# First stage of a fused block: expansion split around the next tile's transposes, ScalarE's and VectorE's order changed

## The reference

```
x = x + tanh(g_xattn[0]) * xattn0(layernorm(x), ctx)     # per tile: scores = k^T q / 16, softmax, times v^T
h = layernorm(x)
z = h @ ternary(W_syn).T + b_syn                          # 128 x 1024 per tile
thresh = 102nd largest z of each row
hidden = where(z >= thresh, relu(z), 0)
x = x + tanh(g_ffn[0]) * (layernorm(h + hidden @ ternary(W_out).T + b_out) * gamma + beta)
x = x + tanh(g_xattn[1]) * xattn1(...)                    # convolution by Toeplitz matrices
x = x + tanh(g_ffn[1]) * mixture_of_experts(...)          # 64 experts, 6 per row
```

## Time and profile before

| what | us |
|---|---|
| median of three runs | 753.64 |
| the profiled execution, device time | 755.16 |
| its span (first to last instruction) | 753.0 |
| first expansion starts | 32.90 |
| second expansion starts | 41.84 |
| twelfth expansion starts | 104.82 |
| last expansion ends | 130.65 |
| threshold search on VectorE starts from the counts | 138.7 |

### The profile page before, as it was taken

One profiled execution on the slowest core, in us unless ns is written; L12 is line 12 of the kernel. 1 busy time (PEld: TensorE's weight loads), 2 busy tenths in 40 slices (PEclk: granted clock), 3 DMA queues, 4 the chain that ended last, 5 costly groups with the idle time before them and its releaser, 6 DMA issues.

```text
span 753.0 us, 12159 instructions
## 1 busy us (share of the span) xinstructions
PE 620.4 (82%) x3072; PEld 475.3 (63%) x3072; DVE 478.6 (64%) x1604; ACT 284.2 (38%) x641; POOL 433.4 (58%) x482
## 2 busy tenths in 40 slices
PE   3698997475699867799999658999999999999930
PEld 2354553243687755677777546788888888888720
DVE  4887777899587777778888352444444535354425
ACT  2135667785134341344555402223332323232200
POOL 2477888321044441377777660667777777777660
PEclk9599999788799997899999978999999999999975
DMA  6347553586568946466764368999999999998858
GB/s 227 109 161 235 190 195 138 194 301 249 200 248 317 328 168 222 159 211 226 247 235 144 125 219 275 288 249 243 245 250 252 245 253 259 260 256 171 228 85 308
DMA packets 89035, 167.84 MB, mean 223 GB/s; under 512 B 11280, under 2 KB 53712, under 8 KB 88976
## 3 DMA queue, kind: packets, MB, share of 16 engines
q1 hardware_dynamic: 67504, 138.44, 55.2%
q0 software_dynamic: 20608, 27.82, 18.8%
q10 hardware_dynamic: 864, 0.93, 0.3%
HBM read 93.33 MB, written 73.81 MB: 222 GB/s over the span
## 4 chain that ended last, share of the span: by engine, by line
PE 63%; DVE 13%; issue 8%; DMA 7%; POOL 3%; ACT 3%; SPq 1%; DVEq 1%; POOLq 0%; ACTq 0%
PE psum L1100 10%; PE psum L863 8%; PE psum L1018 6%; PE psum L1113 6%; PE psum L939 5%; PE psum L1104 5%; PE psum L1084 3%; PE psum L1118 3%; DMA acc<-hh,toki 3%; PE psum L1029 3%; DVE hh L1650 3%; PE psum L975 2%; POOL acc L806 2%; PE psum L835 2%; PE psum L930 2%
## 5 line engine op out<-in xcount | busy, mean ns | idle before, releaser
L806 POOL DMA_INDIRECT acc<-hh,toki x128 | 187.9, 1468 | 83.3 <-DVE hh L1965 47.8
L1965 DVE TENSOR_SCALAR hh<-psum,wtok 96x256 f32<-96x256 f32 (+3 forms) x128 | 55.9, 478 | 133.4 <-issue 113.2
L766 POOL DMA_INDIRECT xs_rows<-Z,slot x96 | 96.3, 1003 | 41.9 <-issue 26.0
L1100 PE MATMUL psum<-qT,Z 128*128 128x192 f32 (+3 forms) x480 | 99.3, 350 | 0.0
L1100 PEld LDWEIGHTS psum<-qT,Z 128*128 128x128 f32 x480 | 81.8, 192 | 3.0 <-issue 0.2
L684 POOL TENSOR_TENSOR rstd<-mv,neghalf 128x1 f32<-128x1 f32 (+1 forms) x48 | 36.8, 767 | 77.5 <-DVE mv L1438 77.5
L1375 ACT ACTIVATE qT<-psum 128x384 f32<-128x384 f32 (+3 forms) x64 | 33.5, 524 | 97.0 <-PE psum L1084 96.2
L863 PE MATMUL psum<-wt,hTs 128*128 128x512 f32 x128 | 62.0, 629 | 8.2 <-ACT hTs L1198 8.2
L939 PE MATMUL psum<-wt,hh 128*128 128x256 f32 x256 | 58.4, 382 | 0.0
L1113 PE MATMUL psum<-Z,hh 128*96 128x256 f32 (+3 forms) x240 | 56.7, 379 | 0.0
L1104 PE MATMUL psum<-qT,Z 128*112 128x192 f32 (+3 forms) x240 | 53.5, 345 | 0.0
(11 more groups left out here) (347 smaller groups left out, 1254.0 us busy)
## 6 DMA issues: line engine op xcount, KB each, us to landing
Z<-in_wexp SPq DMA_DIRECT2D x62, 496.0 KB, 4.3
xs_rows<-fill SPq DMA_DIRECT2D x64, 272.0 KB, 3.2
kv_rows<-Z SPq DMA_DIRECT2D x12, 688.0 KB, 3.8
kvb<-kv_rows SPq DMA_DIRECT2D x8, 688.0 KB, 5.6
Z<-co_rows SPq DMA_DIRECT2D x8, 688.0 KB
Z<-kv_rows SPq DMA_DIRECT2D x8, 688.0 KB, 6.4
Z<-xs_rows SPq DMA_DIRECT2D x24, 204.0 KB, 4.2
Z<-xs_rows SPq DMA_DIRECT2D x16, 272.0 KB, 3.7
```

What stands on the lines that cost most here:

```text
L766: pool.indirect_dma_start(out=xs_rows[:, :], out_offset=bass.IndirectOffsetOnAxis(ap=slot[:, t, k:k + 1], axis=0), in_=H[:, t, :], in_offs ...
L806: pool.indirect_dma_start(out=acc[a][:, :], out_offset=bass.IndirectOffsetOnAxis(ap=toki[0:p, g, j:j + 1], axis=0), in_=y_sb[0:p, s, j, :] ...
L1100: m = pe.matmul(pA[par][:, g * CAP:g * CAP + 2 * p], w[:, s, k, g * P:(g + 1) * P], xT[:, par, k, 0:2 * p], start=(k == 0), stop=(k == 1))
L1965: m = dve.tensor_scalar(y_sb[0:p, s, j, :], pY[par][0:p, j * D:(j + 1) * D], wtok[0:p, g, j:j + 1], None, ALU.mult)
```

## The change

TensorE's expansion of a tile becomes two calls: its first half (columns 0 to 511) stays at the head of the block, its second half goes behind the transposes of the next tile. ScalarE runs X, then C, then EH, with the counts for one tile later than before, and the counts left over follow the loop. On VectorE the instructions stay the same; `link` is taken apart, so that the wait for a result can stand later than the instruction that makes it (`mark` returns the number to wait for), and the block's order is new.

```diff
-            def expand(b, par):
-                pe.wait_ge(hT_ready, b + 1)
-                if later(b):
-                    pe.wait_ge(z_ready, b - 1)
-                for c in range(2):
-                    for k in range(2):
...
+            def expand(b, par, c):
+                if c == 0:
+                    pe.wait_ge(hT_ready, b + 1)
+                    if later(b):
+                        pe.wait_ge(z_ready, b - 1)
+                for k in range(2):
...
+                if c == 1:
+                    m.then_inc(z_done, 1)
...
                 if there(b - 3):
-                    expand(b - 3, 1 - par)
+                    expand(b - 3, 1 - par, 0)
...
                     turn(b - 2, par)
+                if there(b - 3):
+                    expand(b - 3, 1 - par, 1)
...
+            def counts(t):
...
+                first_count(t)
+                if t:
+                    second_count(t - 1)
+
+            for b in range(NT + 2):
+                if b < NT:
+                    soft(b, b % 2)
...
                 if b >= 5:
-                    second_count(b - 5)
...
+                    counts(b - 5)
+                if b >= 2:
+                    evac_h(b - 2, b % 2)
+            for t in range(NT - 3, NT):
+                counts(t)
             second_count(NT - 1)
...
+            def mark(ins):
 
                 v["k"] += 1
                 ins.then_inc(v_step, 1)
-                dve.wait_ge(v_step, v["at"] + v["k"])
+                return v["at"] + v["k"]
...
                 if there(b):
-                    highest(b, par)
+                    reduced = highest(b, par)
                 if there(b - 1):
                     add1(b - 1, 1 - par)
+                if there(b):
+                    exponent_shift(b, par, reduced)
+                if there(b - 1):
+                    summed = stats1(b - 1)
+                if there(b - 2) and early != NT + 1:
+                    norm_h(b - 2, par)
+                if there(b - 1):
+                    aggregated = aggregate1(b - 1, summed)
+                if early == 5:
+
+                    dve.wait_ge(rstd_ready, 4)
+                if there(b):
+                    divided = divisors(b, par)
+                if there(b - 1):
+                    variance1(b - 1, aggregated)
+                if there(b + 2):
+                    query(b + 2, par)
+                if there(b):
+                    scale_v(b, par, divided)
                 if there(b - 4):
                     keep_z(b - 4, par)
```

More of the change, by code:

```diff
@@ L855, in turn @@
                 m.then_inc(hT_full, 1)
-            def expand(b, par):
-                pe.wait_ge(hT_ready, b + 1)
-                if later(b):
-                    pe.wait_ge(z_ready, b - 1)
-                for c in range(2):
-                    for k in range(2):
-                        m = pe.matmul(psum[:, 4 + 2 * par + c, :], hTs[:, par, k, :], wsyn[:, k, c * 512:(c + 1) * 512],
-                                      start=(k == 0), stop=(k == 1))
-                m.then_inc(z_done, 1)
+            def expand(b, par, c):
[4 more added lines that the diff above has]
+                for k in range(2):
+                    m = pe.matmul(psum[:, 4 + 2 * par + c, :], hTs[:, par, k, :], wsyn[:, k, c * 512:(c + 1) * 512],
+                                  start=(k == 0), stop=(k == 1))
+                if c == 1:
+                    m.then_inc(z_done, 1)
             def first_blocks(b, par):
@@ L1198, in evac_h @@
                 act.activation(hTs[:, par], psum[:, 3, 0:D].rearrange("p (k c) -> p k c", k=2), ACT.Copy).then_inc(hT_ready, 1)
[L1200 to L1204, removed]
             def first_done(t):
@@ L1230, in second_count @@
                 ahead_count(2 * t + 2 if t < NT - 1 else 2 * NT - 1, t, thr_2, cnt_2)
-            def ahead(b):
-                if b == 4:
+            def counts(t):
+                if t == 0:
                     act.wait_ge(wabs_ready, 1)
                     act.wait_ge(thr_ready, 1)
-                if b >= 4:
-                    first_count(b - 4)
-                if b >= 5:
-                    second_count(b - 5)
[L1241 to L1251, removed]
+                first_count(t)
[4 more added lines that the diff above has]
+                    soft(b, b % 2)
+                if b == 0:
+                    act.wait_ge(wraw_in, 16)
+                    act.activation(hidden[:, :, :], wraw[0], ACT.Abs, accum_out=wabs[:, 0:1]).then_inc(wabs_ready, 1)
+                if b >= 5:
+                    counts(b - 5)
[3 more added lines that the diff above has]
+                counts(t)
             second_count(NT - 1)
@@ L1408, in _, with link @@
             v = {"at": 0, "k": 0}
-            def link(ins):
+            def mark(ins):
                 v["k"] += 1
                 ins.then_inc(v_step, 1)
-                dve.wait_ge(v_step, v["at"] + v["k"])
+                return v["at"] + v["k"]
+            def link(ins):
+                dve.wait_ge(v_step, mark(ins))
             def tiles(lo_, hi_, per, body):
@@ L1505, in highest, with exponent_shift, divisors, scale_v @@
                 dve.wait_ge(sc_done, b + 1)
-                link(dve.tensor_reduce(smax[:, :], psum[:, par, :].rearrange("p (e d) -> p e d", e=2), AX.X, ALU.max))
+                return mark(dve.tensor_reduce(smax[:, :], psum[:, par, :].rearrange("p (e d) -> p e d", e=2), AX.X, ALU.max))
+            def exponent_shift(b, par, reduced):
+                dve.wait_ge(v_step, reduced)
                 dve.tensor_scalar(nsmax[:, par, :], smax[:, :], -1.0 / 16, None, ALU.mult).then_inc(smax_ready, 1)
-            def scale_v(b, par):
+            def divisors(b, par):
                 dve.wait_ge(attn_ready, b + 1)
+                return mark(dve.reciprocal(rsum[:, :], asum[:, par, :]))
+            def scale_v(b, par, divided):
                 dve.wait_ge(ctx_in[par], 16 * (b - par) + 32)
-                link(dve.reciprocal(rsum[:, :], asum[:, par, :]))
+                dve.wait_ge(v_step, divided)
                 for e in range(2):
@@ L1520, in add1, with stats1, aggregate1, variance1 @@
                 m.then_inc(x1_done, 1)
+            def stats1(b):
                 dve.wait_ge(x1_done, b + 1)
-                moments(X[:, b, :], b, var2_ready)
+                alone(dve, "dve")
+                return mark(dve.bn_stats(stats[:, 0, :], X[:, b, :]))
+            def aggregate1(b, summed):
+                dve.wait_ge(v_step, summed)
+                alone(dve, "dve")
+                return mark(dve.bn_aggr(mvt[:, 0, :], stats[:, 0, :]))
+            def variance1(b, aggregated):
+                dve.wait_ge(v_step, aggregated)
+                dve.tensor_tensor(mv[:, b, :], mvt[:, 0, :], eps2[:, :], ALU.add).then_inc(var2_ready, 1)
             def norm_h(b, par):
@@ L1567, in first_blocks @@
                     first_point()
-                if there(b - 2) and early != NT + 1:
-                    norm_h(b - 2, par)
                 if early == NT - 2:
```

## The result

The change makes the kernel faster: 744.59 us (744.11 to 745.30, four runs) against 753.51 (753.25 to 754.62) for the kernel before on the same chip; the ratio on record is 0.987 with a 95% interval of 0.9856 to 0.9884 (the two medians by themselves give 0.988). The forecast was 745.1, its range 741.5 to 751. A second measurement on another chip gave 744.18 against 753.87, 0.987 [0.985, 0.989].

The account below looks back on a forecast made before the run. The first stage was taken as bound by TensorE with one hole per tile; head +0.1, ten middle tiles -5.2 and end -3.4 made -8.5, from 753.64 to 745.1 us, range 741.5 to 751.

Parts of the forecast that it names:

- one hole: TensorE, after each tile's transposes: idle 0.47 us for the copy out of PSUM, 0.62 per tile with a 0.15 drain.
- the drain: End of TensorE's expansion: 0.15 of its 3.70 us is emptying that a following matmul would cover, leaving 3.55.
- The special tiles: Middle stretch: block 5 with input statistics charged 0.4 us, the long tile waiting for a load 1.1.
- the rival that I gave 0.07: Load: GpSimd stands 4.8 us instead of 2.8, a score waits too; up to 2 more, 747, chance 0.07.
- rival of no effect: The hole moves whole from the copy to the mix, tiles stay at 6.15, the end loses its 3.4: 753.6, chance 0.06.
- meetings with GpSimd: VectorE instructions slowed beside GpSimd's: bounds nothing to 2.7 us per tile, 0.1 charged.
- the mix's circle: From one mix through A, N, exponentials, Rc, V, Q and SV to the next: 4.1 us, 1.4 less than 5.53.
- the second rival's: Second in the rivals' list: the load decides, the long tile costs up to 2 us more, 747, chance 0.07.
- the third's: Third in the rivals' list: VectorE becomes the bound at 7.1 us per tile, about 759, chance 0.05.
- The head: Stage start: first expansion 0.7 us later, the first gap gives 0.62 back, net +0.1 (0 to +1).
- The end: From the ten middle tiles to the last K: 22.5 us instead of 25.86, so -3.4.
- the wait for the late maximum: Tile without scores, near the end: TensorE waits 0.9 us, from VectorE's 2.28 reduction less 1.4 of slack.

Follow-up runs that it names:

- p1_split: Kernel before with only TensorE's expansion split, ScalarE and VectorE in the old order: 754.97 us, ratio 1.0007 to the kernel before.
- p4_split_dve: Changed kernel with ScalarE put back in its old order, TensorE's split and VectorE's new order kept: 756.12 us, ratio 1.0026 to the kernel before.
- d1_k_early: Changed kernel with K put back ahead of the reciprocal on VectorE: 749.83 us, ratio 0.9946 to the kernel before.
- v1_load: Changed kernel with the output weights loaded in four quarters, blocks 8 to 11, behind the small loads: 741.89 us, ratio 0.9844 to the kernel before.
- v3_both: Changed kernel with output weights loaded in quarters and VectorE's weight sums in two halves, blocks 14 and 15: 741.51 us, ratio 0.9831 to the kernel before.
- after_again: The changed kernel unaltered, measured once more on another chip: 744.18 us, ratio 0.987 to the kernel before.

## Why the prediction was right

**The bound and the split.** That a tile is TensorE's work with one hole held, and so did the claim that the second half hides the copy: no expansion but the first waits for it. The size was a little off: the plain tile was put at 5.53 plus 0.1, and it is 5.38. The step at fault is the drain: I took eight steps as 8 x 0.444 = 3.55, but the chain has the eight records in 3.44, 0.43 each. More of the 3.70 was drain than the 0.15 I charged, and the mix lost its own (0.89 to 0.86). Ten tiles by 0.25 are 2.5 us that I did not forecast.

**The special tiles** took nearly as much back. I charged 0.4 for the input statistics and 1.1 for the load, 1.5; the trace has 1.06 and 2.28, 3.34. So 57.14 = 53.8 + 3.34 against 57.8 = 56.3 + 1.5: two misses of opposite sign, and that the total came so close (745.1 for 744.59) is in part luck. The load's part is, in part, the rival that I gave 0.07: GpSimd stood 3.90 (I had said 4.8), and a score waited 1.06 for its own load. What the rival did not have is the echo, three tiles in which GpSimd's lateness puts its products on SV or Q.

**ScalarE's order** was costed at nothing and hides as said. But I did not see how much hangs on it. The prediction asked what the copy's new place might cost; p1_split and p4_split_dve show that without it the hole moves whole to the mix. That was my rival of no effect (753.6), and to the split alone it is what happens.

**VectorE's order** is the step that failed in kind, though not in the sum. I charged it 0.1 per tile for meetings with GpSimd and credited it with nothing. The sum contained its benefit without naming it: the mix's circle left K out because K stands at the end. The prediction put that circle at 4.1 us, with 1.4 to spare, and there it was mis-sized. In the plain tile of the changed kernel the pair of SV is this row,

```profile
93.74 0.47 DVE L1521 TENSOR_SCALAR hh<-ctxT_s,rsum 128x128 f32<-128x128 f32 x2
```

ended at 94.21, and the mix starts at 94.95. With the 0.11 between the two in block 5, about 0.6 of slack is left (an estimate), half of K's 1.27. One term is missing from the sum: it names V but adds nothing for it. From the reciprocal to SV it has 0.20 + 0.41, and p4_split_dve, with V and Q between them, 0.83. d1_k_early gives K's price, 5.7 us at most, paid in blocks where VectorE is late; its plain tiles are 5.38 to 5.55. The charge of 0.1 was put in the wrong place: no plain tile pays it. That the three tiles behind the load pay 0.98 (part of the 2.28), about the 1.0 of ten tiles at 0.1, is coincidence.

The Trainium skill's rule in "SBUF — State Buffer", section "Who interferes with whom", says that a VectorE instruction in a two-port mode, or one with two SBUF inputs beside a GpSimd instruction that reads SBUF, and the GpSimd instruction block each other for the whole of whichever came first. The trace agrees in kind: SV's pair goes from 0.48 to 1.49 beside products, K (one input in PSUM) stays at 1.27 to 1.28; no row shows in which mode SV ran. Whether they meet hangs here on how the two lists stand to each other: in v1_load SV is never stretched. The prediction calls the sum with a meeting each time the second rival's; by its own 2.7 per tile it is the third's, about 759.

**The head.** The first expansion starts 0.5 later (0.7 forecast), but the next gap gives 1.9 back, not 0.6. Before, nearly all of the eight records of the first expansion ran at half rate, 32.90 to the scores at 39.26, 6.36; now four do (33.40 to 36.78, 3.38), and the other four come behind the transposes at 1.72. That 1.26 was not in the sum, and executions differ in it: the first gap between transposes is 6.29 in v1_load, 7.27 in v3_both and 7.54 in after_again. In after_again the slow stretch lasts longer, and from the first expansion (33.42) to the second (41.70) are 8.28, 0.66 less than before, where 0.6 was forecast. Nor does it reach the end of the stage. SV of block 5, late behind the input statistics, ends at 49.28 in the one execution and at 49.31 in the other; where the head was short, the mix waits for it, where it was long, there is no wait (gaps 6.44 and 5.39). From the first transposes to the fourth the two take 18.13 and 18.30, against 21.52 before. So most of the 1.06 that I book for block 5 above is this 1.26 given back.

**The end** held term by term: 5.38, 5.64, 3.88, 3.65 and 3.63 against 5.63, 5.57, 3.8, 3.8 and 3.7, and the wait for the late maximum 0.88 against 0.9.

**The signs.** As forecast, GpSimd no longer waits for H, and the copy waits for the transposes. VectorE's wait for the exponentials, which I expected to stay, shrank from 7.6 us in nine waits to 1.4 in six. TensorE idle before the mix is there in block 5 and in the tiles behind the load, where by the times of the rows SV released it late, and before the last mix.

## What to carry to other kernels

Before an instruction is split to cover a wait, follow, through every engine's list, the circle that is left when the wait is gone: here the next consumer stood behind two counts on ScalarE, and the split alone was worth nothing. A long instruction that nobody waits for (K) belongs behind the short ones that the bound engine needs; its price showed here almost only in blocks that were late for another reason. Where two engines disturb each other, a stall can cost more than its own tile (here 1.30 there and 0.98 behind it): look at the tiles behind it.

## What the runs showed of the hardware

The granted clock in a windows row and the rate of the records can disagree. For 33.40 to 36.60 us of the changed kernel's first execution the row gives 1.00, the full level, yet the weight loads there take 0.34 with 0.52 idle before each, and from 39.16 on, with the same 1.00 in the row, 0.19 with 0.24:

```profile
33.40:36.60 3.20, 3.20 (x4) 1.48 (x5) 2.81 (x14) 0.76 (x4) 3.20 (x6) 1.00 0.03 7
...
35.24 0.34 PEld L863 LDWEIGHTS psum<-wt,hTs 128*128 128x128 f32 x1 [0.52 <-issue]
...
39.16 0.19 PEld L863 LDWEIGHTS psum<-wt,hTs 128*128 128x128 f32 x1 [0.24 <-issue]
```

In after_again the same stretch has the granted clock at 0.50, half level, with records as slow. TensorE had stood idle for 5.38 us before the first mix at 30.36. So at the head of this stage I trust the records, not the clock column.

In the tile of the one transfer of the output weights, which stands ahead of the small loads in SyncE's queue, the DMA engines were busy throughout, and the loads behind it came 1.06 and 3.90 us too late; in quarters behind them (v1_load) neither was waited for. The window of that tile (columns as above, the last two DMA share and GB/s):

```profile
61.09:67.77 6.68, 5.62 (x20) 3.13 (x19) 4.97 (x13) 4.05 (x10) 2.78 (x5) 1.00 1.00 381
```
